# An attention and expert kernel: statistics a batch earlier, and POOL making the modulation product and the causal mask

## What is computed

```python
mod = (_silu(L0_c) @ L0_wmod).reshape(L0_c.shape[0], 6, 1, -1)
sa, ca, ga, sb, cb, gb = (mod[:, 0], ..., mod[:, 5])
h = _layernorm(x, axis=-1) * (1 + ca) + sa
x = x + ga * _L0_attn_ref(h, W_q, W_k, W_v, W_o)     # q, k = elu(.) + 1, causal sum of k v, divided by z . q
h = _layernorm(x, axis=-1) * (1 + cb) + sb
x = x + gb * _L0_ffn_ref(h, ...)                     # layer norm, router, top 2 of 8, GELU experts 256 -> 1024 -> 256
```

## Time and profile before

| | us |
|---|---|
| median of 3 runs (lowest, highest) | 1125.11 (1123.71, 1125.61) |
| the profiled execution | 1125.48 |
| its span | 1123.6 |
| PE busy | 988.9 (88%) |
| DVE busy | 889.1 (79%) |
| POOL busy | 573.6 (51%) |
| ACT busy | 542.9 (48%) |

### The profile page before, as it was taken

How to read it: one execution, slowest core, us unless ns; L and a number is a source line. 1 busy time by engine, 2 the same in 40 slices (tenths; PEclk the granted TensorE clock), 3 DMA queues, 4 the chain that set the end, 5 groups by cost and what they waited for, 6 DMA issues and landing times.

```text
span 1123.6 us, 31567 instructions
## 1 busy us (share of the span) xinstructions
PE 988.9 (88%) x8116; PEld 806.3 (72%) x8117; DVE 889.1 (79%) x3010; ACT 542.9 (48%) x1123; POOL 573.6 (51%) x478
## 2 busy tenths in 40 slices
PE   5777879887945099999999999999999999999997
PEld 1334545554534088888888888888888888888875
DVE  5578999999985567777877877877877877877776
ACT  1668787878843134434444443444443443444443
POOL 2121666666667536655455445445445445545543
PEclk8798888888965599999999999999999999999999
DMA  4465777876869466665565555566555556566453
GB/s 134 133 227 194 237 230 260 291 271 212 315 233 401 122 185 132 137 123 92 96 118 98 106 112 104 98 109 99 94 108 103 90 108 108 87 120 122 88 100 49
DMA packets 162626, 169.80 MB, mean 151 GB/s; under 512 B 89340, under 2 KB 136968, under 8 KB 158472
## 3 DMA queue, kind: packets, MB, share of 16 engines
q1 hardware_dynamic: 129736, 114.24, 36.5%
q0 software_dynamic: 32832, 54.88, 25.3%
HBM read 94.67 MB, written 62.78 MB: 140 GB/s over the span
## 4 chain that ended last, share of the span: by engine, by line
PE 66%; issue 8%; DVE 8%; POOL 6%; ACT 2%; DMA 1%; POOLq 0%; DVEq 0%; SPq 0%; ACTq 0%
PE banks L1440 32%; PE banks L1452 31%; POOL lists L551 5%; PE banks L1334 2%; DVE st L771 2%; POOL rs L544 2%; DVE store L968 1%; PE banks L1322 1%; ACT rowbuf L628 1%; DVE mv L779 1%; ACT store L712 1%; DVE rowbuf L908 1%; DMA out<-rowbuf,ydst 0%; DVE store L926 0%; DVE ix L1001 0%
## 5 line engine op out<-in xcount | busy, mean ns | idle before, releaser
L1440 PE MATMUL banks<-nhl,store 128*128 128x256 bf16 (+1 forms) x3408 | 450.5, 268 | 28.0 <-DMA nhl<-xhl 24.8
L740 ACT ACTIVATE gf<-banks,b1t 128x256 f32<-128x256 f32 (+1 forms) x568 | 263.0, 463 | 429.1 <-PE banks L1440 411.7
L1452 PE MATMUL banks<-store 128*128 x3240 | 448.0, 273 | 0.5
L1440 PEld LDWEIGHTS banks<-nhl,store 128*128 x3408 | 324.1, 98 | 71.0 <-issue 30.1
L587 POOL DMA_INDIRECT out<-rowbuf,ydst x135 | 223.7, 1657 | 294.1 <-DVE rowbuf L1222 222.0
L1452 PEld LDWEIGHTS banks<-store 128*128 128x128 bf16 x3240 | 310.5, 98 | 41.9 <-issue 1.8
L1231 DVE CAST store<-gf 128x256 bf16<-128x256 f32 (+1 forms) x568 | 180.5, 318 | 130.7 <-ACT gf L740 99.3
L1233 DVE TENSOR_TENSOR store<-gf,store 128x256 bf16<-128x256 f32 (+1 forms) x568 | 234.7, 413 | 19.5
L551 POOL DMA_INDIRECT lists<-store,slot x128 | 141.0, 1102 | 96.3 <-issue 49.0
L578 POOL DMA_INDIRECT store<-y_rows,ygb x135 | 135.2, 1001 | 63.3 <-issue 51.8
L544 POOL TENSOR_TENSOR rs<-ve,mhalf 128x12 f32<-128x12 f32 (+2 forms) x20 | 39.0, 1950 | 84.6 <-DVE ve L786 84.5
(11 more groups left out here) (225 smaller groups left out, 970.0 us busy)
## 6 DMA issues: line engine op xcount, KB each, us to landing
rowbuf<-lists SPq DMA_DIRECT2D x64, 264.0 KB
store<-in_L_ffn_w SPq DMA_DIRECT2D x16, 1024.0 KB, 6.0
wsplit<-store SPq DMA_DIRECT2D x16, 1024.0 KB, 5.7
store<-wsplit SPq DMA_DIRECT2D x16, 1024.0 KB, 11.1
b2t<-in_L_ffn_b SPq DMA_DIRECT2D x71, 128.0 KB
store<-in_L_attn_x SPq DMA_DIRECT2D x16, 512.0 KB, 9.6
out<-store SPq DMA_DIRECT2D x16, 512.0 KB, 9.9
csB<-mod_rows SPq DMA_DIRECT2D x16, 256.0 KB, 4.0
```

The source lines that it names most:

```text
L740: a.activation(gf[:, c % 2, 0:halves(j) * P], MM[c % 2][:, 0:halves(j) * P], ACT.Gelu, bias=b1t[:, r, c:c + 1]).then_inc(gf_s, 1)
L1440: last = t.matmul(MM[c % 2][:, 0:halves(j) * P], w, nhl[:, r, m, 0:halves(j) * P], start=n == 0, stop=n == 5)
L1452: last = t.matmul(ACC[r][h][:, 0:D], g[:, c, h * P:(h + 1) * P], w, start=c == 0 and n == 0, stop=c == NI - 1 and n == 2)
```

## The change

It has four parts.
1. The statistics of x run two batches ahead instead of one: those of batches 0 and 1 are taken before the steps begin, and step i takes those of batch i+2. SP loads batch i+3 in step i (batches 2 and 3 in step 0). All counts of statistics, powers and nm shift by one.
2. ACT makes xc of batch i+1 in step i, behind the copies for the output product (xc of batch 0 before the steps, of batch 1 in the middle of step 0), instead of xc of batch i at the start of step i.
3. POOL makes the product (was L901) and the causal mask (was L886), in this order, between wog and the first four scatters. DVE keeps the addition, which now waits for POOL's product.
4. The router's bias (was L858) moves from the preparations into DVE's step 0, behind phi and its products; PE waits for it only ahead of the first scores.

```diff
-            return slice(0 if i < NB else 1 if i - 3 < NB else 2, 1 if i < 3 else 2 if i < 4 else 3)
+            return slice(0 if i + 1 < NB else 1 if i - 3 < NB else 2, 1 if i < 3 else 2 if i < 4 else 3)
...
             def load_x(i, half, r):
...
+                for b in range(2 if i == 0 else i + 3, min(i + 4, NB)):
+                    sp.wait_ge(got_x[b % 2], 16 * (b // 2))
+                    sp.dma_start(resid[:, b * NC:(b + 1) * NC, :], x_v[b]).then_inc(got_x[b % 2], 16)
...
             def inverse_root(i, r):
-                pool.wait_ge(ve_s, i + 1)
-                wait_past(pool, xc_s, upto(i - 1))
+                pool.wait_ge(ve_s, i + 2)
+                wait_past(pool, xc_s, upto(i))
...
+            inverse_root(-1, 1)
             inverse_root(0, 0)
...
+                if norm:
+                    b, q = i - 3, 1 - r
+                    pool.wait_ge(got_cs[q], 16 * (half if q == 0 else half - 1))
+                    pool.wait_ge(xn2_s, b + 1)
+                    wait_past(pool, nrm_s, b - 1)
+                    g.tensor_tensor(h2[q], xn2, csB[:, q, D:2 * D].unsqueeze(1).to_broadcast([P, NC, D]), ALU.mult).then_inc(h2m_s, 1)
+                if attend:
+                    pool.wait_ge(strip_s, i)
+                    diag = pt[:, :].rearrange("p (a t) -> p a t", a=NC)[:, :, 0:P]
+                    g.tensor_tensor(diag, diag, causal[:, :].unsqueeze(1).to_broadcast([P, NC, P]), ALU.mult).then_inc(diag_s, 1)
                 if place:
                     pool.wait_ge(slot_s, i - 4)
                     pool.wait_ge(w1_s, i - 4)
...
+            def centred(b, r):
+                act.wait_ge(got_x[b % 2], 16 * (b // 2) + 16)
+                wait_past(act, xT_s, b)
+                normalise(lambda c: xc[:, c, :], rows(b), r, 0, xc_s)
+            act.wait_ge(nm_s, 1)
+            centred(0, 1)
...
-                if project:
-                    act.wait_ge(got_x[r], 16 * half + 16)
-                    wait_past(act, xT_s, i)
-                    normalise(lambda c: xc[:, c, :], rows(i), r, 0, xc_s)
...
+                if i == 0:
+                    centred(1, 0)
...
+                if 0 < i < NB - 1:
+                    centred(i + 1, r)
...
             def step(i, half, r, project, attend, settle, norm, route, place):
                 taken = stats_before(i)
...
-                if attend:
-                    b = i - 1
-                    dve.wait_ge(strip_s, b + 1)
-                    diag = pt[:, :].rearrange("p (a t) -> p a t", a=NC)[:, :, 0:P]
-                    v.tensor_tensor(diag, diag, causal[:, :].unsqueeze(1).to_broadcast([P, NC, P]), ALU.mult).then_inc(diag_s, 1)
...
+                if i + 2 < NB:
+                    dve.wait_ge(got_x[r], 16 * half + 32)
                     hold(dve, "dve")
-                    stats(rows(i + 1), 0)
+                    stats(rows(i + 2), 0)
                 if norm:
                     b, q = i - 3, 1 - r
                     dve.wait_ge(got_cs[q], 16 * (half if q == 0 else half - 1))
-                    dve.wait_ge(xn2_s, b + 1)
-                    wait_past(dve, nrm_s, b - 1)
+                    dve.wait_ge(h2m_s, b + 1)
                     hold(dve, "dve")
-                    v.tensor_tensor(h2[q], xn2, csB[:, q, D:2 * D].unsqueeze(1).to_broadcast([P, NC, D]), ALU.mult).then_inc(h2m_s, 1)
+                    v.tensor_tensor(h2[q], h2[q], csB[:, q, 0:D].unsqueeze(1).to_broadcast([P, NC, D]), ALU.add).then_inc(h2_s, 1)
...
+                if i == 0:
+                    router_bias()
```

More of the change, by code:

```diff
@@ L821, in _ @@
             moments(0, 0)
-            var_eps(0, 1)
+            var_eps(-1, 1)
+            dve.wait_ge(got_x[1], 16)
+            dve.wait_ge(mv_s, 1)
+            hold(dve, "dve")
+            stats(rows(1), 0)
+            neg_mean_rstd(-1, 1)
+            dve.wait_ge(nm_s, 1)
+            dve.wait_ge(ve_s, 1)
+            moments(0, 1)
+            var_eps(0, 2)
             dve.wait_ge(mod_ps, 1)
@@ L854, in _, with router_bias @@
             v.tensor_copy(ef[:, 0, 0:1], base[:, 0:1]).then_inc(base_set, 1)
-            dve.wait_ge(rb_ps, 1)
-            dve.wait_ge(got_r, 32)
             dve.wait_ge(base_set, 1)
-            v.tensor_tensor(rbias[:, :], rbias[:, :], S[1][:, 0:E], ALU.add).then_inc(setup_done, 1)
-            dve.wait_ge(setup_done, 1)
+            hold(dve, "dve")
             v.tensor_copy(lge[:, :], lngb[:, 0, :]).then_inc(lge_s, 1)
+            def router_bias():
+                dve.wait_ge(rb_ps, 1)
+                dve.wait_ge(got_r, 32)
+                v.tensor_tensor(rbias[:, :], rbias[:, :], S[1][:, 0:E], ALU.add).then_inc(setup_done, 1)
+                dve.wait_ge(setup_done, 1)
             def step(i, half, r, project, attend, settle, norm, route, place):
                 taken = stats_before(i)
-                dve.wait_ge(nm_s, i + 1 if not isinstance(i, int) else min(i + 1, NB + 4))
+                dve.wait_ge(nm_s, min(i + 2, NB + 5))
                 if settle:
@@ L1327, in step @@
                     pe.wait_ge(vT_s, b + 1)
+                    if b == 0:
+                        pe.wait_ge(setup_done, 1)
                     wait_past(pe, x2_s, b)
```

32 lines of the change are left out of this document (7 added, 25 removed).

## The result

| | before | after |
|---|---|---|
| median of 4 runs (lowest, highest), us | 1125.14 (1123.71, 1125.61) | 1160.61 (1159.03, 1161.59) |
| the profiled execution (its span) | 1125.48 (1123.6) | 1159.03 (1157.2) |
| DVE, POOL, ACT busy | 889.1, 573.6, 542.9 | 904.5, 631.0, 543.0 |

The ratio is 1.0316, with a 95% interval of 1.0298 to 1.0334: slower by 35.5 us, where the forecast was 8 (range 1117 to 1141). DVE was relieved of some 30 us of work (sixteen masks of 0.68 us and sixteen products of 1.21) and is busy 15 us longer.

What follows compares the result with a forecast made beforehand. It took a loop between DVE and POOL in the attention stage as the bound; -3.1 + 5.3 + 1.3 + 2.0 + 0.6 + 2.4 = +8.5, rounded to +8, against 1125.48 us gave about 1133.5 us, range 1117 to 1141.

Steps and rivals of the forecast that it cites:

- the loop: Attention steps: DVE's slots release POOL's scatters and power, which nm needs before the next slots; 9.5 plus 9.57 us.
- prices of POOL's work: Product and mask on POOL, priced from the wog row: 2.4 us and 1.3 us.
- A: Step after an odd step's nm: product holds the port shared with DVE, delaying ohs; 2.0 us lost, 1.15 gained.
- B: Step after an even step's nm: product on POOL holds DVE's pick at the shared port; 1.4 us lost, 1.15 gained.
- gain of 1.15 us a step from slots to nm: POOL's half: without L901 stretching a scatter, slots to nm takes 8.35 us instead of 9.5.
- 2.30 for the power: POOL's inverse root after four scatters, ahead of nm: assumed to take 2.30 us of the 8.35.
- second rival: POOL slower: product 2.96, mask 1.48, plus waits for DVE's scan or L940; 1141 us, chance 0.14.
- The start: Steps 0 to 5: batch 2's load delays the first phi by 4.8 us, later gains leave -3.1.
- third rival: Start goes otherwise: 4.1 us not absorbed, 1137.5; never arising, 1129.5, or 1125 with a cheaper port; chance 0.12.
- Steps 15 to 17: Late attention steps: no scatter gain in 15 and 16, one product in 17; +1.3, +2.0 and +0.6 us.
- The end: After step 17 POOL scatters without pause: of the last two products one fits, one adds 2.4 us.
- first rival: Port costs DVE nothing, as its small instructions slip in ahead of the product; about 1119 us, chance 0.27.

Runs made afterwards that it cites:

- e5: The changed kernel, with POOL's product waiting until wog has ended and its mask until the product has ended; ratio to before 1.0164.
- e4: The changed kernel with x of batches 2 and 3 loaded among SP's preparations, ahead of its wait for the modulations; ratio to before 1.0151.
- e7: e3 with two products of constants, results never read, added on POOL behind wog; ratio to before 1.0512.
- e3: The changed kernel with both product and mask given back to DVE; ratio to before 1.0044.
- e9: e3 with e4's early load, the mask on POOL behind the wait for slots, and three scatters instead of four ahead of the power; ratio to before 0.9928.

## Why the prediction was wrong

The direction, the loop and the kind of loss were right. How long the loss lasts was not, and with it the size: 35.5 us instead of 8.

**The loop and the prices of POOL's work** held. The product took 2.35 us (forecast 2.4) and the mask 1.26 (1.3). The trace agrees with the estimate of 2.3 us from the figure of the Trainium skill's page "GPSIMD Engine Reference", section "Performance versus the Vector engine". Without L901 beside it the second scatter takes 1.18 us instead of 1.72, so the scatter's stretch was indeed DVE's. By the rule of the Trainium skill's page "SBUF — State Buffer", section "Who interferes with whom", it would not have been; the measurement decides, and the rule does not hold here.

**The port loss in A was forecast as 2.0 us, and in B as 1.4.** They were 2.96 (12.46 against 9.50) and 3.75 (12.68 against 8.93), which is 3.3 of the 4.2 us that the forecast of a pair was short. This is the step that failed most: "It gets the port at the latest when oh ends at 6.07, and holds it until 8.27", and for B "oh and ohs are past". I took each POOL instruction as one hold, after which DVE gets its turn. But the next one is in line before the last has ended, and DVE waits for the whole row: 3.15 us for dl in A, up to 4.7 for oh or ohs in B. In e5, where there are gaps, A loses 2.06 us, nearly the 2.0 of the forecast, and B 2.17; ohs is held for 2.24 us there as forecast, but beside it d for 1.10 and not pick, so that the nearness is partly luck. In after it is dl that is held in A, not ohs. For B the forecast overlooked its own row: ohs at 222.72, held for 0.64 us by a wog that starts 0.15 ahead of it, is that of a B step. In after wog starts 6.01 us after the power's end, as forecast, and ohs at 6.16.

Two sums were also off: 6.07 to 8.27 leaves 2.2 us for a product priced at 2.4, which makes the forecast 1 us short, and 35.0 and 2.15 make a first phi at 37.15, not 37.3.

**The gain of 1.15 us a step from slots to nm** was 0.82 in A and 0.47 in B. The term that failed is "2.30 for the power". It starts earlier after slots, as forecast, and is now behind the scan's start instead of ahead of it: 3.04 us. That POOL could wait for the scan stood in the second rival, but without a price of its own and with all of it under 0.14. With both, a pair is 5.3 us longer (21.62 against 18.96 a step, twice 2.66), where 1.1 stood; over nine steps 23.9 instead of 5.3.

**The start** was right in its parts and wrong at its end. phi of step 0 came at 36.90 (37.3), nm of step 5 was 3.3 us early (3.4), and nm of step 6 was only 0.1 early where 3.1 were to remain: between the two d was held for 2.17 us by the product and w1 for 0.99 by the mask, so that the slots came only 0.7 us early; then POOL's first scatter waited 2.26 us after the mask had ended (the trace doesn't show for what), and the power started at 119.17, where before's stood at 119.20. The forecast had put this hold at 0.3 us, on dl. The third rival, batch 2 in time, I priced at 4 us; e4 gives 8.8, since the forecast had left out that DVE's 4.9 us of waiting for the router's bias were gone as well.

**Steps 15 to 17** cost 7.3 us instead of 3.9: from nm to slots they lose 3.35, 2.54 and 2.56 us, where 1.3, 2.0 and 0.6 stood, and from slots to nm they gain 1.2 in all. **The end** cost 2.1 us instead of 2.4. The sum by the measured terms is -0.1 + 23.9 + 7.3 + 2.1 = 33.2.

Of the signs that were named, DVE idle ahead of nm in each step came (27.5 us in 14 times), and so did the wait for a DMA (9.99 us) and the product at 2.3 to 2.6. "Pairs of 38 to 39 us" failed, and so did the signs of who is held: ohs near 2.2 us in every second step (it is 4.15 to 4.17 in three of the B steps and 0.19 in the others), and pick over 0.5 (0.2; w1 or d is held instead).

The first rival, that the port costs nothing, is refuted by e7: 59 us for two products that nobody waits for, against e3.

## What to carry to other kernels

Work moved from VectorE to GpSimd is not off VectorE's path when VectorE's next instructions are small ones with both inputs in SBUF: each waits for all of GpSimd's row, so price the row, not the instruction, and price it against the half of the loop into which it falls. If such work must be there, put a wait between its instructions, or place it where VectorE does statistics or reads PSUM, which were not held here; in e9 that made the mask harmless, not useful. And where two instructions are 0.2 us apart in the forecast, take both outcomes. Don't count on being first: dl started ahead of wog and was held for the whole row, and in B it made no difference of note whether oh was held (4.71 us) or got through and left ohs to be held (0.47 and 4.15): the ways from nm to slots differ by 0.35 us.
